# Third attention by pairs of batches, with a new order of the first loads

## The reference

```
Q = norm @ Wq.T + bq ;  K = ctx @ Wk.T + bk
attn = softmax(Q @ K.T / sqrt(512)) ;  out = attn @ ctx
```

## Time and profile before

| what | value |
|---|---|
| median of 3 runs | 1538.02 us (1536.37 to 1538.24) |
| the profiled execution | 1535.57 us |
| its span on the core | 1533.8 us |
| mean granted TensorE clock | 0.941 |
| PE, DVE, ACT, POOL busy | 89%, 73%, 44%, 22% |
| first attention | to some 424 us |
| second attention's scores and outputs | some 461 to 590 us |
| third attention | some 662 to 704 us |
| third feed-forward's first products | 717.9 us |

### The profile page before, as it was taken

One profiled execution on the slowest core, in us unless ns is written; L12 is line 12 of the kernel. 1 busy time (PEld: TensorE's weight loads), 2 busy tenths in 40 slices (PEclk: granted clock), 3 DMA queues, 4 the chain that ended last, 5 costly groups with the idle time before them and its releaser, 6 DMA issues.

```text
span 1533.8 us, 18726 instructions
## 1 busy us (share of the span) xinstructions
PE 1370.0 (89%) x6532; PEld 985.8 (64%) x6532; DVE 1121.2 (73%) x2045; ACT 676.8 (44%) x1403; POOL 336.4 (22%) x380
## 2 busy tenths in 40 slices
PE   6999999999997989987999998999999999999104
PEld 5665566566575658664788875777777777778102
DVE  4788898888888986946555567566566566667998
ACT  3777777777424434422222224444343443443104
POOL 1112112212163020321211111221212212122520
PEclk9999999999999989966999999999999999999557
DMA  5578988789710011512221310201101012000001
GB/s 214 151 170 185 238 219 198 172 212 221 209 42 1 1 56 34 106 35 49 49 69 54 102 69 1 69 28 43 43 27 69 28 42 69 1 1 1 0 0 56
DMA packets 37831, 127.76 MB, mean 83 GB/s; under 512 B 4928, under 2 KB 10944, under 8 KB 31536
## 3 DMA queue, kind: packets, MB, share of 16 engines
q1 hardware_dynamic: 26224, 83.38, 15.9%
q0 software_dynamic: 11520, 43.26, 14.8%
HBM read 72.63 MB, written 10.75 MB: 54 GB/s over the span
## 4 chain that ended last, share of the span: by engine, by line
PE 59%; DVE 22%; ACT 6%; DVEq 5%; DMA 4%; issue 2%; POOL 1%; SPq 1%; POOLq 0%
PE PS L150 12%; PE PS L152 11%; PE PS L151 11%; DVE AR L672 4%; PE PS L921 4%; PE PS L959 4%; DMA AR<-AR 3%; ACT s_sb L605 2%; DVE AR L2557 2%; PE PS L945 2%; DVE AR L2546 2%; DVE AR L2553 2%; DVEq L662 1%; DVE AR L678 1%; PE PS L266 1%
## 5 line engine op out<-in xcount | busy, mean ns | idle before, releaser
L436 POOL DMA_DIRECT2D AR<-AR x76 | 75.1, 1117 | 346.3 <-DMA AR<-AR 133.6
L151 PE MATMUL PS<-R16r 128*128 128x512 f32 (+1 forms) x328 | 122.1, 372 | 0.0
L508 PE MATMUL PS<-R,HT 128*128 128x256 f32 x512 | 116.5, 381 | 3.2 <-ACT R L594 2.7
L533 PE MATMUL PS<-R,PT 128*128 128x512 f32 x256 | 116.1, 596 | 3.4 <-DVE X L712 3.4
L152 PE MATMUL PS<-R16r 128*128 128x512 f32 (+1 forms) x312 | 119.1, 382 | 0.0
L508 PEld LDWEIGHTS PS<-R,HT 128*128 128x128 f32 x512 | 94.7, 190 | 16.2 <-ACT R L594 4.6
L1079 ACT COPY AR<-PS 128x512 f32<-128x512 f32 x64 | 37.5, 585 | 146.3 <-PE PS L152 145.8
L605 ACT ACTIVATE s_sb<-PS,sm 128x64 f32<-128x64 f32 x256 | 77.9, 336 | 53.1 <-DVE sm L697 52.6
L150 PE MATMUL PS<-HTr,R16r 128*128 128x512 f32 (+1 forms) x240 | 89.9, 374 | 3.0 <-DVE R16r L190 1.6
L150 PE MATMUL PS<-R16r,HTr 128*128 128x512 f32 (+1 forms) x224 | 90.2, 403 | 0.0
L152 PE MATMUL PS<-HTr,R16r 128*128 128x512 f32 (+1 forms) x240 | 87.4, 364 | 0.0
(11 more groups left out here) (311 smaller groups left out, 3574.7 us busy)
## 6 DMA issues: line engine op xcount, KB each, us to landing
AR<-AR POOLq DMA_DIRECT2D x76, 528.0 KB, 6.6
OR<-in_wo SPq DMA_DIRECT2D x12, 1024.0 KB, 12.2
dequantised<-AR SPq DMA_DIRECT2D x8, 1056.0 KB, 5.5
WR<-in_w0q SPq DMA_DIRECT2D x8, 1024.0 KB, 12.2
AR<-in_w3q SPq DMA_DIRECT2D x8, 1024.0 KB, 5.1
WR<-dequantised SPq DMA_DIRECT2D x22, 256.0 KB, 2.8
AR<-in_nf SPq DMA_DIRECT2D x4, 1056.0 KB, 9.3
nf_in<-in_nf SPq DMA_DIRECT2D x4, 1056.0 KB, 10.5
```

The source lines that it names most:

```text
L151: nc.tensor.matmul(out, ah, bl, start=False, stop=False)
L436: nc.gpsimd.dma_start(nf_below(g)[:, part], what[:, part], accum_op=ALU.add, max_dma_last_dim=4 * N_NF // 2).then_inc(added, 16)
L508: i = nc.tensor.matmul(bank(2 + u % 2)[:, tt * 256:(tt + 1) * 256], HT0[:, c, tok], m[:, :, c * B + b, :], start=c == 0, stop=c == C - 1)
L533: i = nc.tensor.matmul(bank(5 + tt), PT[:, at:at + P], vo[:, pr, b, :], start=pr == 0, stop=pr == 1)
```

## The change

1. **Loads.** SP issues CT, WKV0, X tiles 0 and 1 (512 KB), X tiles 2 to 7 (1536 KB), WQ0, then as before. DVE waits for the second part of X after its first pair of statistics.
2. **Gates.** The tanh moves from the front of ACT's list to behind the copies of pieces 5 to 8.
3. **Second attention.** `project_q(1, 0)` moves ahead of norm tiles 6 and 7.
4. **POOL.** `pool_f2(1)` moves behind norm pair 2 of norm 4.
5. **Bias.** BK is made as two columns of 128 keys (eight matmuls with one moving column) in place of a row of 256 (four matmuls).
6. **Scores.** For a pair of batches, M2's 64 columns of each batch are stationary and 256 tokens of HT0 stream, to the lower and upper 64 partitions of one bank (`products`, eight matmuls). ACT copies with the bias added, two transposes turn the result back to tokens (`scores`).
7. **Outputs.** PT now has two batches on 128 partitions: two transposes for a half in place of four. The context CB lies on 128 partitions; outputs go to banks 0, 1, 2, 7 in the order 0, 2, 1, 3, taking rows 0 to 63 and 64 to 127 in turn.
8. **DVE's order.** The norm scalings of tiles 6, 7 go ahead of the first softmax shift; sums, statistics and norm 5 are interleaved.

```diff
             stat(0)
+            if n == 0:
+                dve.wait_ge(x_rest_in, 16)
             stat(1)
...
+                if t == 2:
+                    act.wait_ge(consts_in, CONSTS)
+                    nc.scalar.activation(tg[:], gates[:], ACT.Tanh).then_inc(gates_ready, 1)
...
             scores(0)
+            pe.wait_ge(lo_ready, T + 4)
+            project_q(1, 0)
             pe_norm_tile(pe, 2, 6)
             pe_norm_tile(pe, 2, 7)
-            project_q(1, 0)
             scores(1)
...
-            pool_f2(pool, (0, 1))
+            pool_f2(pool, (0,))
             pool_norm_pair(pool, 4, 2)
+            pool_f2(pool, (1,))
             pool_norm_pair(pool, 4, 3)
             accumulate(pool, LATE, 4)
             pool_norm(pool, 5)
...
-                for dc in range(C):
-                    i = nc.tensor.matmul(bank(6)[0:1, 0:256], b2[:, dc:dc + 1], KT2[:, dc * 256:(dc + 1) * 256],
-                                         start=dc == 0, stop=dc == C - 1)
+                for p in range(2):
+                    for dc in range(C):
+                        at = dc * 256 + p * P
+                        i = nc.tensor.matmul(bank(6)[:, p:p + 1], KT2[:, at:at + P], b2[:, dc:dc + 1],
+                                             start=dc == 0, stop=dc == C - 1)
...
+            def products(h):
+                pe.wait_ge(hi_ready, T * 4 + 4 * h + 4)
...
+                for c in range(C):
+                    for bb in range(2):
+                        b = 2 * h + bb
+                        i = nc.tensor.matmul(bank(TURNED_BANKS[h])[SK * bb:SK * (bb + 1), 0:S],
+                                             M2[:, c * 256 + b * SK:c * 256 + (b + 1) * SK],
+                                             HT0[:, c, b * S:(b + 1) * S], start=c == 0, stop=c == C - 1)
+                i.then_inc(A2["s_mm"], 1)
...
-            for t in range(6):
-                scores(t)
+            products(0)
             pe_f2_turn(pe, 0, 0, 0)
             pe_f2_turn(pe, 0, 0, 1)
+            scores(0)
             pe_norm_tile(pe, 4, 6)
             pe_norm_tile(pe, 4, 7)
-            scores(6)
-            scores(7)
+            products(1)
             pe_f2_turn(pe, 0, 0, 2)
+            scores(1)
             turn_p(0)
             outputs(0)
             turn_p(1)
             outputs(1)
...
-            exps(0)
+            turned_scores(0)
             act_f2_high(act, 0, 0, 0)
             act_f2_high(act, 0, 0, 1)
             act_norm(act, 4, (6, 7))
+            exps(0)
+            turned_scores(1)
             act_f2_high(act, 0, 0, 2)
...
-            shift(0)
             norm_scaled(dve, 4, 6)
             norm_scaled(dve, 4, 7)
+            shift(0)
             dve_f2_low(dve, 0, 0, 0)
+            norm(0)
             dve_f2_low(dve, 0, 0, 1)
-            norm(0)
             dve_f2_low(dve, 0, 0, 2)
             shift(1)
+            sums((0, 1))
+            norm(1)
             down(dve, LATE, 4)
-            norm(1)
-            for t in range(T):
-                sum_tile(dve, A2, 2, 0, (0, 1), t)
-            dve_stats(dve, PAIRS - 1)
+            sums((2, 3))
+            dve_stats(dve, 0)
+            sums((4, 5))
+            dve_stats(dve, 1)
+            norm_scaled(dve, 5, 0)
+            norm_scaled(dve, 5, 1)
+            sums((6, 7))
+            dve_stats(dve, 2)
+            norm_low(dve, 5, 0)
+            norm_low(dve, 5, 1)
+            norm_scaled(dve, 5, 2)
+            norm_scaled(dve, 5, 3)
+            dve_stats(dve, 3)
...
-            sp.dma_start(X[:], x_d.rearrange("(t p) n -> p t n", p=P)).then_inc(x_in, 16)
-            sp.dma_start(CT[:], ctxT_d).then_inc(ctx_in, 16)
+            x_tiles = x_d.rearrange("(t p) n -> p t n", p=P)
+            sp.dma_start(CT[:], ctxT_d).then_inc(A0["kv_in"], 16)
             sp.dma_start(WKV0, wkv_d[0]).then_inc(A0["kv_in"], 16)
+            sp.dma_start(X[:, 0:2], x_tiles[:, 0:2]).then_inc(x_in, 16)
+            sp.dma_start(X[:, 2:T], x_tiles[:, 2:T]).then_inc(x_rest_in, 16)
```

More of the change, by code:

```diff
@@ L1855, in act_f1 @@
             act.wait_ge(A2["m_mm"], 1)
-            nc.scalar.copy(BK, bank(6)[0:1, 0:256])
-            nc.scalar.copy(M2, bank(0, 2)).then_inc(A2["m_ready"], 1)
+            nc.scalar.copy(BK, bank(6)[:, 0:2])
+            nc.scalar.copy(M2, bank(0, 2)).then_inc(A2["keys_ready"], 1)
             act.wait_ge(F1["gap"], 1)
@@ L1957, in dve_f1 @@
             dve_stats(dve, PAIRS - 1)
-        CB = AR[0:SK, 0:B * D]
+        CB = AR[:, 0:2 * D]
         KT2 = WR[:, 2048:2048 + C * B * SK]
@@ L1972, in pe_a2, with scores @@
         def pe_a2(pe):
[L1973 to L1979, removed]
-                nc.tensor.matmul(o, ones[0:1, :], BK[:, b * SK:(b + 1) * SK], start=True, stop=False)
-                for c in range(C):
-                    m = slice(c * 256 + b * SK, c * 256 + (b + 1) * SK)
-                    i = nc.tensor.matmul(o, HT0[:, c, tok], M2[:, m], start=False, stop=c == C - 1)
+            def products(h):
+                pe.wait_ge(hi_ready, T * 4 + 4 * h + 4)
+                if h == 0:
+                    pe.wait_ge(F1["acc"], 6)
+                for c in range(C):
+                    for bb in range(2):
[4 more added lines that the diff above has]
+                i.then_inc(A2["s_mm"], 1)
+            def scores(h):
+                pe.wait_ge(A2["turned_copied"], h + 1)
+                for tt in range(2):
+                    cols = slice(tt * P, (tt + 1) * P)
+                    i = nc.tensor.transpose(scores2(h)[:, cols], turned2(h)[:, cols], ident[:])
                 i.then_inc(A2["s_mm"], 1)
@@ L1987, in turn_p @@
                 pe.wait_ge(A2["probs"], h + 1)
-                for t in range(4):
-                    i = nc.tensor.transpose(bank(2 + h)[0:SK, t * P:(t + 1) * P], half2(h)[:, t * SK:(t + 1) * SK], ident[:])
+                for tt in range(2):
+                    cols = slice(tt * P, (tt + 1) * P)
+                    i = nc.tensor.transpose(bank(2 + h)[:, cols], half2(h)[:, cols], ident[:])
                 i.then_inc(A2["t_mm"], 1)
@@ L1994, in outputs @@
                 pe.wait_ge(A2["b_in"], 16)
-                for t in range(4 * h, 4 * h + 4):
-                    if t >= 2:
-                        pe.wait_ge(A2["acc"], t - 1)
-                    b = t // 2
-                    nc.tensor.matmul(bank(t % 2), PT[0:SK, t * P:(t + 1) * P], CB[:, b * D:(b + 1) * D],
-                                     start=True, stop=True).then_inc(A2["mm"], 1)
-            for t in range(6):
-                scores(t)
+                for k in range(4 * h, 4 * h + 4):
+                    if h:
+                        pe.wait_ge(A2["acc"], k - 3)
+                    t = OUT_ORDER[k]
+                    tt, bb = t % 2, t // 2 % 2
+                    rows = slice(SK * bb, SK * (bb + 1))
+                    nc.tensor.matmul(bank(OUT_BANKS[k]), PT[rows, h * 256 + tt * P:h * 256 + (tt + 1) * P],
+                                     CB[rows, h * D:(h + 1) * D], start=True, stop=True).then_inc(A2["mm"], 1)
+            products(0)
             pe_f2_turn(pe, 0, 0, 0)
             pe_f2_turn(pe, 0, 0, 1)
+            scores(0)
             pe_norm_tile(pe, 4, 6)
             pe_norm_tile(pe, 4, 7)
-            scores(6)
-            scores(7)
+            products(1)
             pe_f2_turn(pe, 0, 0, 2)
+            scores(1)
             turn_p(0)
@@ L2015, in act_a2, with turned_scores @@
         def act_a2(act):
+            def turned_scores(h):
+                act.wait_ge(A2["s_mm"], 2 * h + 1)
+                nc.scalar.activation(turned2(h), bank(TURNED_BANKS[h])[:, 0:S], ACT.Identity, bias=BK[:, h:h + 1])\
+                    .then_inc(A2["turned_copied"], 1)
             def exps(h):
@@ L2663, in _ @@
         def _(act):
-            act.wait_ge(consts_in, CONSTS)
-            nc.scalar.activation(tg[:], gates[:], ACT.Tanh).then_inc(gates_ready, 1)
             act_x0(act)
@@ L2738, in lay_out @@
         'ctxT': chunks(ctxf.T),
-        'ctxB': f['ctx_4096'].transpose(1, 0, 2),
+        'ctxB': f['ctx_4096'].reshape(2, P, D).transpose(1, 0, 2),
         'gx': f['g_xattn'].reshape(1, 4), 'gf': f['g_ffn'].reshape(1, 4),
```

43 lines of the change are left out of this document (23 added, 20 removed).

## The result

The changed kernel took 1509.69 us (median of 4 runs, 1509.37 to 1511.66) against 1538.13 (1536.37 to 1540.18) for the one before on the same chip: ratio 0.9827, 95% interval 0.9806 to 0.9848, 28.4 us less. The forecast was 1519.8 with a range of 1512 to 1528: right in direction, too small by 10 us, and just outside the range. The profiled execution took 1511.66 us; its span is 1509.9, 23.9 shorter than that of before.

The account below looks back on a forecast made before the run. PE, busy 89% of the span, was taken as near the bound except in three short places; 4.3 + 1.5 - 0.2 + 8.0 + 4.6 = 18.2 us off 1535.6 gave 1517.4, median 1519.8, range 1512 to 1528.

Parts of the forecast that it names:

- The first rival: First attention, paced by a loop on a DMA, gives the start's 4.3 us back: 1524; chance 0.17.
- slower: First attention: accumulating DMAs and weight loads share a queue and lengthen each group's chain, some 1541; chance 0.04.
- no-effect: Whole kernel: all gains lie on PE while another engine decides, 1538; chance 0.03.
- The second rival: Third and second attention: clock returns early, 10.7 and 3.0 us for 8.0 and 1.5, 1515.6; 0.25 of the likeliest.
- place three: Third attention, 661 to 718 us: PE busy at granted clock 0.51, then DVE's serial work until the feed-forward.
- The start: Kernel start: new load order and moved tanh bring fold_queries from 19.48 to 15.2, gaining 4.3 us (3.3 to 5.0).
- Second attention: project_q(1, 0) moved into PE's wait: DVE starts on scores(1) 1.2 to 3.0 us sooner, 1.5 taken.
- I take 8.0: Third attention: scores by pairs bring the last mask 6.3 to 10.7 us sooner, 8.0 taken.
- POOL's 1.1: Third attention: block 1 scaled behind norm pair 2 starts norm tiles 4, 5 1.1 us sooner, inside the 8.0.
- After the mask: Mask to the feed-forward's first products: 28.5 us becomes 23.9, gaining 4.6 (3.4 to 7.0).
- The rival that POOL's block grows: Norm 5 waits for POOL, not DVE, throughout; up to 3 us less gain, 1523; chance 0.12.
- the 0.3 that I had tried: Third attention: a drain of 0.3 us per tiling-mode change would cost 2 us over six; by the row nothing.

Follow-up runs that it names:

- only_loads: The kernel before with only the new order of loads and the moved tanh (changes 1 and 2); 1530.66 us, ratio 0.9962.
- undo_a1: The changed kernel with project_q(1, 0) behind norm tiles 6 and 7 again, the second attention's old order; 1515.21 us, ratio 0.9865.
- before_filled: The kernel before with four unread products of 512 columns in TensorE's waits ahead of norm 4's tiles; 1534.81 us, ratio 0.9984.
- pool_only: The kernel before with only GpSimd's order changed, block 1 scaled behind norm pair 2; 1532.16 us, ratio 0.9970.
- undo_pool: The changed kernel with block 1 scaled ahead of norm pair 2 again on POOL; 1512.26 us, ratio 0.9836.
- mask_later: The changed kernel with the last mask behind two low parts of block 1 and POOL's DMAs behind norm 5; 1507.36 us, ratio 0.9809.
- rows_in_turn_off: The changed kernel with outputs in order 0 to 7, so two neighbours use the same 64 rows; 1511.61 us, ratio 0.9832.
- after_again: The changed kernel, unchanged, timed once more on the chip of the later runs; 1512.02 us, ratio 0.9835.
- after_filled: The changed kernel with nine unread products in TensorE's waits of norm 5; 1508.52 us, ratio 0.9822.
- later_filled: The changed kernel with mask_later's order, a1_filled's unread products and seven more in norm 5's waits; 1506.52 us, ratio 0.9789.
- a1_filled: The changed kernel with six unread products of 256 columns in TensorE's waits before the second attention's scores(1); 1512.09 us, ratio 0.9832.

## Why the prediction was too small

**What bounds the kernel** was right: three short places, the long stretches handing a gain on. The first rival (the start given back) is wrong: only_loads has 5.0 us at the start, 5.7 at the end of the first attention and 6.2 at the end of the second. The slower and the no-effect cases fall with the result; the adding DMAs and the weight loads of the slower case aren't in one queue either, GpSimd starts the former and SP the latter. The second rival (the clock returns early in place three) was right in what it said of the clock there, and its 10.7 us for the mask were still too few; its other half, the scores of the second attention at full clock, didn't come.

**The start**: 4.9 for 4.3, and 5.9 at the end of the first attention. The parts of X and the weights came 0.5 to 1.2 us earlier than reckoned (5.74 for 6.9, 7.16 for 8.2, 11.49 for 12.0), as the order of the queue has it.

**Second attention**: 2.5 to 2.7 for 1.5, by undo_a1 against after. The half clock of `scores(1)` was right (3.75 us, reckoned 3.8); the term left out what the earlier start spared behind it: DVE's product over SBUF takes 1.23 us where it took 2.34 before, since POOL's long instruction (469.99 to 474.58 in after) is all but over when it comes at 474.53. In undo_a1 it takes 2.35 us again, beside POOL's instruction from 471.73 to 476.29. In the kernel before, that instruction ran from 476.81 to 481.37, and DVE's product beside it was this row:

```profile
480.11 2.34 DVE L358 TENSOR_TENSOR s_sb<-s_sb,sm 128x1024 f32<-128x1024 f32 x1
```

**The step that failed** is "I take 8.0, nearer the slow end, because the granted clock of this stretch was 0.51". I read the clock of the old score tiles as that of the new code. Measured, in the two traces: 6.9 us at the end of the second attention, 11.2 at the norm tiles 4 and 5, 22.8 at the mask. The term of 8.0, with bounds of 6.3 and 10.7, measured 15.9. From 11.2 to 22.8 is 11.5 us (unrounded); the sum had 8.0 less POOL's 1.1 for it, 6.9. Even its full-clock end, 9.6, was too low, since it kept the norm tiles and the first products at half clock (5.4 us; measured 3.6). Three things were mis-sized:

- The products run at full clock, in all nine profiles that have them with POOL's new order: 1.95 us for sixteen records, against 3.5 in my sum at half clock and 1.75 at full. The price itself was good to 0.2.
- The half clock wasn't even fixed for the old code. With the wait ahead filled (before_filled), gone (pool_only) or still there (only_loads), four, three and three score tiles run at 1.10 us, and the stretch up to A2's start is 6.9, 7.7 and 5.0 us shorter than in before. Of the 10.9 us that after gains there, 5 to 8 are thus clock and POOL's order, and 3 to 6 are left for the pairs of batches and the rest (an estimate from one profile each). Why the new products keep the clock stays open: no run has them with 64 columns, and the waits of 1.9 and 0.6 us ahead are the same in both kernels. In undo_pool, with 2.49 us of idle time just before, the first products take 3.11 us. POOL's order, which I had put at 1.1 us, is worth 1 to 3 in the new code and, taken alone, 4.5 in the medians.
- 4.3 us came ahead of the norm tiles, where the sum had 1.1: the wait for POOL is gone, the last wide product before them takes 1.88 us for 3.27 at full clock, and the code ahead of it, which is the same in both, took 1.8 us less. Only the first of the three is the change's for certain: the wide product takes 3.09 and 3.12 us in mask_later and rows_in_turn_off, whose code up to it is that of after, and the part ahead of it gains 0.2 us in only_loads and 1.6 in pool_only. I had taken the 3.27 for that product's price; most of it was at half clock.

**After the mask**: 4.6 forecast, 3.4 measured at F2's start (4.7 at the first products, of which 1.3 were lost because they are at half clock up to the ninth, in before up to the third). POOL's 8.3 us and the scaling released by POOL came as told. The rival that POOL's block grows is wrong.

**Products side by side, and changes of mode.** The outputs ran side by side, eight records in 1.99 us, where four took 1.98. The Trainium skill (TensorE: Matmul & The Clock Gate, Part 3) has products with few rows in different row groups run together, and the trace agrees. That section of the Trainium skill also has products start and end strictly in the order of the program. rows_in_turn_off doesn't fit that: there four records in the same rows stand ahead of the third output, they alone took 1.98 us in the earlier trace rows, and yet all eight start in four pairs and are done in 1.99. A change of mode cost next to nothing: the products with 64 stationary columns start 0.56 us after the four transposes ahead of them (651.57 to 652.13), and a product that keeps the 128 columns starts 0.46 after its four (648.08 to 648.54). By the Trainium skill (TensorEngine Tiling (Array Packing), Key Properties) each change of tiling mode drains the engine; if it does, the drain costs at most 0.1 us here, not the 0.3 that I had tried in the prediction.

**What remains.** 23.9 us in the traces leaves 2.3 us that were there at F2's start (26.2) and gone at the end; only_loads had the opposite sign (10.1, then 13.5). The code behind is the same, the mean granted clock there is 0.91 in both, and its drops lie elsewhere in each profile. That these 2 to 3 us are such drops is argued, not shown. And 4.5 us of the difference between the medians is the choice of the executions profiled: by after_again, against 17 runs of before, all of the change is 24.6 us (0.9809 to 0.9861), nearer to the 23.9 and 25.5 of the spans. The sum from rows, 18.2, was short of these by 6 to 7. The rest of the miss is the spread of single runs (before alone: 1532.7 to 1543.5), which my range, made from one profile's terms, didn't hold; after_again's median of 1512.02 lies at its low end. Of the signs named in the prediction, the start, the second attention, DVE's idle time and the scaling released by POOL came; the products at 3.5 us and the feed-forward's first products near 700 (690.42) didn't.

## What to carry to other kernels

A clock read from the stretch that a change replaces says little of the new code, and one profile says little of the old: the same score tiles took 1.97 us each in one execution and 1.10 in another. Read the clock from several executions, and reckon both levels as two cases; that the waits ahead are the switch isn't shown here. A wait on the clocked engine can cost more than its length (undo_pool); look first at what runs on the slow engine (here GpSimd's scaling) just before the result that everyone waits for. A mask that a queue-blocking engine must issue belongs behind the short results that the same engine owes others.

## What the runs showed of the hardware

- TensorE was at 1.2 GHz though never idle: 9.00 of 9.00 us busy at a granted clock of 0.51, with 64-column products behind full loads of weights (pool_only, 663 to 672 us). In the 12 us before it had waited 1.94, 0.57 and 0.56 us.
- The same waits had different answers: the kernel before fell to half clock in the wide product at 657.27, behind waits of 1.94 and 0.57 us (3.27 us); pool_only, with the same two waits, didn't (1.88 us from 655.27).
- With unread products in the waits of norm 5 it stayed nearly always at 2.4 GHz: in after_filled and later_filled the clock of 670 to 690 us is 0.93 and 0.92, in after 0.59:

```profile
670.00:690.00 20.00, 13.70 (x55) 8.09 (x56) 14.80 (x31) 4.86 (x8) 3.56 (x7) 0.93 0.33 76
```

- Outputs of different row groups ran side by side in either order of issue, 1.99 us for eight records, as long as nothing stood between them; with waits between, 4.66 against 3.66 us.
- A DVE instruction with two SBUF operands took 2.89 us beside one of GpSimd and 1.23 alone; one with a PSUM operand took 1.23 beside it too (a1_filled, 470.03 us). The Trainium skill, SBUF — State Buffer, SBUF: two separate sides, gives the cause as a lock on shared ports; the row fits it, since 1.81 us of GpSimd's work were left when it began and it took 1.66 longer.
- Behind two adding DMAs, GpSimd's next result (`rstd`) came 8.3 us after the first began, the same in both kernels to a tenth.
